# Respreading one image's convolution, statistics and group norm over the sampling of the image before it

## The reference, cut to what matters

```python
# block 1: x = x + L0(gn(x))
xh = conv1x1(gn(x), w_in, b_in)                    # 64 -> 128 channels
kernels = kg_w2 @ relu(kg_w1 @ mean(xh) + kg_b1)   # 9 taps per image and channel
y = depthwise_conv3x3(xh, kernels)
y = y * tanh(softplus(y))
x = x + conv1x1(y, w_out, b_out)
# block 2: x = x + L1(gn(x)); gn: mean and variance of two channels over the image
offset, mask = conv3x3(gn(x)), sigmoid(conv3x3(gn(x)))
val = bilinear samples of gn(x) at 9 offset taps per pixel, times mask
z = conv1x1([conv(val, w_def), offset, mask]); x = x + silu(batchnorm(z))
```

## Time and profile before

| | us |
|---|---|
| median of 3 runs | 5547.52 (5545.2 to 5550.46) |
| the profiled execution | 5541.43 |
| its span, first to last instruction | 5539.6 |
| PE busy (81% of the span) | 4466.2 |
| DVE busy (81%) | 4498.5 |
| ACT busy (47%) | 2595.6 |
| POOL busy (73%) | 4041.9 |

### The profile page before, as it was taken

One profiled execution on the slowest core, in us unless ns is written; L12 is line 12 of the kernel. 1 busy time (PEld: TensorE's weight loads), 2 busy tenths in 40 slices (PEclk: granted clock), 3 DMA queues, 4 the chain that ended last, 5 costly groups with the idle time before them and its releaser, 6 DMA issues.

```text
span 5539.6 us, 46074 instructions
## 1 busy us (share of the span) xinstructions
PE 4466.2 (81%) x14774; PEld 1996.3 (36%) x14774; DVE 4498.5 (81%) x5310; ACT 2595.6 (47%) x3580; POOL 4041.9 (73%) x4243
## 2 busy tenths in 40 slices
PE   8688787888878888788887878887778887888874
PEld 3233343433434333333333433333333343333331
DVE  6888969888797887978879798897978879788765
ACT  3354445445445544444554454454445444445321
POOL 1777777777777777777777777777777777777776
PEclk8687878888787887878878788788888878788886
DMA  4334344343534435344343443434344353433433
GB/s 106 103 118 135 103 133 122 120 131 105 141 111 131 123 109 143 104 131 123 116 136 105 133 123 120 133 103 139 115 132 123 110 144 105 131 115 114 122 107 101
DMA packets 280991, 667.35 MB, mean 120 GB/s; under 512 B 76191, under 2 KB 118058, under 8 KB 278506
## 3 DMA queue, kind: packets, MB, share of 16 engines
q0 software_dynamic: 203328, 555.49, 33.7%
q1 hardware_dynamic: 77424, 108.93, 7.9%
HBM read 610.00 MB, written 54.12 MB: 120 GB/s over the span
## 4 chain that ended last, share of the span: by engine, by line
PE 36%; DVE 25%; POOL 22%; issue 12%; ACT 3%; DMA 2%; DVEq 0%; POOLq 0%; SPq 0%; ACTq 0%
POOL gat L504 22%; PE yo_ps L774 12%; PE tap_ps L774 7%; DVE gat L1371 5%; PE z_ps L696 5%; DVE pairs L1350 5%; DVE conv_ps L1241 4%; DVE hat_s L1398 4%; PE tap_ps L690 2%; DMA gat<-patch_table,ixu 2%; PE conv_ps L588 2%; PE conv_ps L568 2%; DVE uc L1248 1%; PE xh_ps L756 1%; DVE conv_ps L1238 1%
## 5 line engine op out<-in xcount | busy, mean ns | idle before, releaser
L504 POOL DMA_INDIRECT gat<-patch_table,ixu x4236 | 4033.6, 952 | 1483.6 <-issue 1261.8
L1371 DVE TENSOR_TENSOR gat<-gat,wgt_ps 128x1024 f32<-128x1024 f32 x1059 | 1283.9, 1215 | 445.9 <-DMA gat<-patch_table,ixu 438.7
L1350 DVE TENSOR_REDUCE pairs<-gat 128x256 f32<-128x1024 f32 x1024 | 1239.4, 1210 | 0.0
L774 PE MATMUL yo_ps<-hat_s,hat_image 128*128 128x512 f32 x1860 | 1007.0, 695 | 7.0 <-issue 7.0
L774 PE MATMUL tap_ps<-hat_s,hat_image 128*128 128x512 f32 x1860 | 895.1, 631 | 0.0
L690 PE MATMUL tap_ps<-ident,pairs 128*128 128x128 f32 x2048 | 393.3, 324 | 572.6 <-DVE pairs L1350 572.4
L1039 ACT ACTIVATE val<-tap_ps 128x512 f32<-128x512 f32 x512 | 303.3, 592 | 1087.9 <-PE tap_ps L690 1087.7
L774 PEld LDWEIGHTS yo_ps<-hat_s,hat_image 128*128 128x128 f32 x1860 | 417.5, 232 | 603.5 <-issue 594.2
L1241 DVE SCALAR_TENSOR_TENSOR conv_ps<-xh,kb,conv_ps 128x1024 f32<-128x1024 f32 x480 | 617.5, 1286 | 12.7
L690 PEld LDWEIGHTS tap_ps<-ident,pairs 128*128 128x128 f32 x2048 | 271.1, 163 | 886.1 <-DVE pairs L1350 716.9
L774 PEld LDWEIGHTS tap_ps<-hat_s,hat_image 128*128 128x128 f32 x1860 | 360.5, 202 | 427.6 <-issue 417.8
(11 more groups left out here) (238 smaller groups left out, 4858.2 us busy)
## 6 DMA issues: line engine op xcount, KB each, us to landing
gat<-patch_table,ixu POOLq DMA_INDIRECT x4236, 2.7
xb<-in_x SPq DMA_DIRECT2D x31, 1024.0 KB, 10.8
patch_table<-rec SPq DMA_DIRECT2D x120, 256.0 KB, 2.6
hat_image<-patch_table SPq DMA_DIRECT2D x144, 128.0 KB
out<-n_z SPq DMA_DIRECT2D x128, 128.0 KB, 2.4
patch_table<-np SPq DMA_DIRECT2D x2, 1072.5 KB
patch_table<-gat SPq DMA_DIRECT2D x8, 256.0 KB, 2.0
patch_table<-rec SPq DMA_DIRECT2D x16, 97.0 KB
```

The source lines that it names most:

```text
L504: pool.indirect_dma_start(gat[:, k, t * 2 * REC:(t + 1) * 2 * REC], None, table_rows, bass.IndirectOffsetOnAxis(ixu[:, i, k, t:t + 1], 0)) ...
L774: m = pe.matmul(hat_sums[t % 2][:, :], hat_image[:, q // NCH % 2, i, t, :], hat_s[:, i, :], start=(i == 0), stop=(i == HI - 1))
L1350: dve.tensor_reduce(total, gat[:, k, :].rearrange("p (t x c h) -> p t c x h", t=TILES, x=2, h=2), mybir.AxisListType.XY, ALU.add).then_inc ...
L1371: dve.tensor_tensor(patch, patch, wk.rearrange("p (n h) -> p n h", h=2).unsqueeze(2).to_broadcast([128, TILES * 2, C, 2]), ALU.mult).then_ ...
```

## The change

Of one image's steps in the chunks of the image before (steady state, images 1 to 15):

- chunk 0: rows of `convolve 0` at units 1, 2 and 4 instead of 2, 3 and 5; `exp`, `ln`, `tanh` of pair 0 at 5, 6, 7; `project 0` at 8 instead of unit 1 of chunk 1.
- chunk 1: `residual 0` alone (its statistics go to chunk 2), three rows of `convolve 1` at 2, 4 and 7, `exp 1` at 8.
- chunk 2: `ln 1`, `tanh 1`, `project 1` at 1, 2, 3, `residual 1` and `statistics 0` at 5, two rows of `convolve 2` at 6 and 8.
- chunk 3: the last row of `convolve 2` at 1, its activation and `project 2` at 2 to 5, `statistics 1`, `residual 2` at 7, the first row of `convolve 3` at 8.
- chunk 4: two rows of `convolve 3` at 1 and 2, activation and `project 3` at 3 to 6, `statistics 2`, `residual 3`, `statistics 3`, and `group_mean` at the end. Before, chunks 0 to 3 held one whole pair each, and chunk 4 the rest and the whole group norm.
- chunk 5: `group_var` and `normalise` at 1 and 2; `last_row` and `offsets 0` at 4 instead of 1; the rest of the preparation moves behind, so that `to_pixels 1` and `to_table 4` pass to chunk 6.
- chunk 7 stays.

In the prologue PE does five of the nine taps instead of six, ACT instead of DVE clips at 20 out of the bank, the activations have four buffers, the statistics and kernels of image 1 go behind the first index, the table uses three banks instead of two, and five copies instead of six are DVE's. `store_last` becomes two transfers: 96 partitions, each with one run of 1024 bytes, and one partition.

```diff
-PE_TAPS = 6
+PE_TAPS = 5
-PLAN_FIRST = ((2, "convolve 0"), (3, "convolve 1"), (5, "convolve 2"), (6, "exp"), (7, "ln"), (8, "tanh"))
-PLAN_BLOCK0 = ((1, "project"), (3, "residual"), (3, "convolve 0"), (4, "convolve 1"), (5, "convolve 2"), (6, "exp"),
-               (7, "ln"), (8, "tanh"), (8, "finish"))
+PLAN_CONV = (
+    ((1, "convolve 0 0"), (2, "convolve 0 1"), (4, "convolve 0 2"), (5, "exp 0"), (6, "ln 0"), (7, "tanh 0"), (8, "project 0")),
+    ((1, "residual 0"), (2, "convolve 1 0"), (4, "convolve 1 1"), (7, "convolve 1 2"), (8, "exp 1"), (8, "finish")),
+    ((1, "ln 1"), (2, "tanh 1"), (3, "project 1"), (5, "residual 1"), (5, "statistics 0"), (6, "convolve 2 0"), (8, "convolve 2 1"), (8, "finish")),
+    ((1, "convolve 2 2"), (2, "exp 2"), (3, "ln 2"), (4, "tanh 2"), (5, "project 2"), (6, "statistics 1"), (7, "residual 2"), (8, "convolve 3 0"),
+     (8, "finish")),
+    ((1, "convolve 3 1"), (2, "convolve 3 2"), (3, "exp 3"), (4, "ln 3"), (4, "statistics 2"), (5, "tanh 3"), (6, "project 3"), (8, "residual 3"),
+     (8, "statistics 3"), (8, "finish"), (KK, "group_mean")),
+)
...
-PLAN_NORM = ((1, "project"), (3, "residual"), (4, "group_mean"), (5, "group_var"), (6, "normalise"), (8, "finish"))
 PLAN_PREPARE = (
-    ((1, "last_row"), (1, "offsets 0"), (2, "to_table 0"), (2, "x_stats 0"), (3, "to_table 1"), (4, "offsets 1"), (4, "to_pixels 0"),
-     (5, "to_table 2"), (5, "x_stats 1"), (6, "to_table 3"), (7, "to_pixels 1"), (8, "to_table 4"), (8, "finish")),
-    ((1, "offsets 2"), (2, "to_table 5"), (2, "points 0"), (3, "offsets 3"), (3, "to_pixels 2"), (4, "points 1"), (4, "to_table 6"),
-     (5, "x_stats 2"), (5, "to_table 7"), (6, "points 2"), (6, "to_pixels 3"), (7, "x_stats 3"), (8, "finish")),
+    ((1, "group_var"), (2, "normalise"), (2, "x_stats 0"), (4, "last_row"), (4, "offsets 0"), (5, "to_table 0"), (5, "x_stats 1"), (6, "to_table 1"),
+     (7, "offsets 1"), (7, "to_table 2"), (8, "to_pixels 0"), (8, "finish"), (KK, "to_table 3")),
+    ((1, "to_table 4"), (1, "offsets 2"), (2, "to_pixels 1"), (3, "to_table 5"), (3, "points 0"), (4, "offsets 3"), (4, "to_table 6"), (5, "points 1"),
+     (5, "to_pixels 2"), (5, "to_table 7"), (5, "x_stats 2"), (6, "points 2"), (7, "to_pixels 3"), (7, "x_stats 3"), (8, "finish")),
...
-                dst = table_rows[bass.ds((n % 2) * (TR * PW) + PIX, 2 * LAST), :].rearrange("(t p) d -> p t d", p=LAST)
-                sp.dma_start(dst, rec_l.rearrange("p (t d) -> p t d", t=2)).then_inc(last_out, 16)
+                first = (n % 2) * (TR * PW) + PIX
+                dst = table_rows[first:first + 2 * (LAST - 1), :].rearrange("(p t) d -> p (t d)", t=2)
+                sp.dma_start(dst, rec_l[0:LAST - 1, :]).then_inc(last_out, 16)
+                dst = table_rows[first + 2 * (LAST - 1):first + 2 * LAST, :].rearrange("(p t) d -> p (t d)", t=2)
+                sp.dma_start(dst, rec_l[LAST - 1:LAST, :]).then_inc(last_out, 16)
...
+            for s in range(NCH // 2):
+                project(0, s, s)
...
+            group_mean(0)
+            group_var(0)
+            first_table(0)
+            first_table(1)
+            offsets(0, 0, 0)
+            last_row(0)
+            for c in range(2, 6):
+                first_table(c)
+            first_pixels(0, 0)
+            first_table(6)
+            first_table(7)
+            x_mean(1)
             x_var(1)
             x_norm(1)
-            group_mean(0)
-            group_var(0)
```

More of the change, by code:

```diff
@@ L115, in plan_of @@
 def plan_of(b, g):
[L117 to L122, removed]
+    plan = PLAN_CONV[g] if g < 5 else PLAN_PREPARE[g - 5]
+    if b == 0 and g < len(PLAN_START):
+        plan = by_unit(plan, PLAN_START[g])
     q = b * NCH + g
@@ L138, in group @@
             done = units
-        name, _, number = step.partition(" ")
+        name, *numbers = step.split()
         if name in steps:
-            steps[name](b, g, int(number or 0))
+            steps[name](b, g, *(int(i) for i in numbers))
     if done < KK:
@@ L1153, in _, with hidden @@
             dve.memset(one_c[:, :], 1.0).then_inc(consts_set, 1)
-            def hidden(n, s):
-                for j in range(2):
+            def hidden(n, s, lo=0, hi=2):
+                for j in range(lo, hi):
                     q = n * NCH + s * 2 + j
@@ L1220, in convolve_first @@
                         dve.scalar_tensor_tensor(acc, src, kb[:, k:k + 1], acc, ALU.mult, ALU.add).then_inc(conv, 1)
[L1221 to L1225 removed]
+                    if k == 0:
+                        hidden(0, NCH // 2 - 1, 1, 2)
             def convolve(n, s, row):
@@ L1262, in residual, with statistics @@
                     dve.scalar_tensor_tensor(own, project_ps(n, j)[:, :], b_out, own, ALU.add, ALU.add).then_inc(x1_done, 1)
+                if n == 0:
+                    statistics(0, s)
+            def statistics(n, s):
+                for j in range(2):
+                    q = n * NCH + s * 2 + j
                     dve.wait_ge(x1_done, q + 2)
-                    dve.bn_stats(stat1[:, bass.ds(s * 2 + j, 1), :].rearrange("p o s -> p (o s)"), own).then_inc(st_done, 1)
+                    dve.bn_stats(stat1[:, bass.ds(s * 2 + j, 1), :].rearrange("p o s -> p (o s)"), xb[:, n % 2, span(s * 2 + j)]).then_inc(st_done, 1)
             def group_mean(n):
@@ L1419, in _ @@
             x_norm(0)
-            for s in range(NCH // 2):
+            for s in range(NCH // 2 - 1):
                 hidden(0, s)
+            hidden(0, NCH // 2 - 1, 0, 1)
             kernels(0)
-            for s in range(NCH // 2):
-                convolve_first(s, s % 2)
-                if s > 0:
-                    project(0, s - 1, (s - 1) % 2)
-                if s > 1:
-                    residual(0, s - 2)
-                x_stats(1, s)
-            x_mean(1)
-            residual(0, NCH // 2 - 2)
-            project(0, NCH // 2 - 1, 1)
+            convolve_first(0)
+            convolve_first(1)
+            x_stats(1, 0)
+            project(0, 0, 0)
+            convolve_first(2)
+            project(0, 1, 1)
+            x_stats(1, 1)
+            convolve_first(3)
+            project(0, 2, 2)
+            residual(0, 0)
+            residual(0, 1)
+            project(0, 3, 3)
+            residual(0, 2)
+            residual(0, 3)
+            group_mean(0)
             step = [0]
@@ L1457, in _ @@
             dve.sem_inc(set_dve, 1)
-            x_var(1)
-            residual(0, NCH // 2 - 1)
-            x_norm(1)
             dve.wait_ge(border_out, 32)
-            group_mean(0)
             group_var(0)
+            x_stats(1, 2)
             normalise(0)
-            for c in BY_DVE:
+            first_table(1)
+            dve.wait_ge(set_pe, 1)
+            then(dve.tensor_copy(w_pair[:, :, :].rearrange("p k c -> p (k c)"), tap_ps[0][:, 0:PAIRS * C]))
+            then(dve.tensor_copy(w_single, tap_ps[0][0:C, PAIRS * C:GROUPS * C]))
+            then(dve.tensor_copy(w_hat[:, :], tap_ps[0][:, GROUPS * C:(GROUPS + 1) * C]))
+            dve.sem_inc(set_dve, 1)
+            x_stats(1, 3)
+            for c in BY_DVE[1:]:
                 first_table(c)
             first_points(0)
+            x_mean(1)
+            x_var(1)
+            x_norm(1)
             kernels(1)
```

186 lines of the change are left out of this document (81 added, 105 removed).

## The result

The changed kernel takes 5686.84 us (median of 4 runs, 5676.02 to 5706.32), the kernel before 5546.36 beside it: ratio 1.026, 95% interval 1.0245 to 1.0274. The profiled execution took 5684.62 us, its span is 5682.8 (before 5539.6).

A forecast was written before the change was run, and what follows sets the result against it. POOL's gather pace bounds the kernel, 330 of 337.2 us an image. Loop 345.2, +8.0 an image: +112 over fourteen, -8 for prologue and image 0, 5645 profiled, median 6.1 above: 5651 us; range 5585 to 5765.

The forecast's parts named there:

- The late norm decides: Chunks 5 to 7: later group norm puts hat_part 60 us after chunk 5's start; to next chunk 0 140.5 us, before 136.5.
- the sum: Loop per image: 207 us for chunks 0 to 4 plus 140.5 us for 5 to 7, 347.5; less 2.3, 345.2.
- The spread chunks: Chunks 0 to 4 on DVE with rows spread: together 207 us, before 202.0.
- The clock: PE, less idle, would be at its higher clock more often: 2.3 us taken off each image.
- The prologue: Ahead of image 0: group mean 8 us earlier, first gather at 107 to 110 us; 8 us gain left after image 0.
- The lag's limit: POOL at chunk 0: waits begin once DVE's first step trails POOL's first gather by more than 24.3 us.
- DVE's slack: DVE's waits for landings in chunks 4 and 5, 19.3 us an image, would fall well below that.
- The waits vanish: Rival: loop through DVE stays below POOL's 330 us, transpose waits go; 5464 us, 5490 with a third left; chance 0.24.
- drain: ACT's table loads: a skill's 1.38 us after each 1.28 us switch; the trace showed none, so none was counted.

The follow-up runs named there:

- the run with the points early: Second chunk's offsets, pixels and points ahead of image 1's hidden layer, against the changed kernel with the previous loop plan: 5532.14 us, 0.9978 of the kernel before.
- rows spread inside their chunk: Rows of convolutions 1 to 3 at units 3, 5, 7 instead of 3, 4, 5, against the changed kernel with the previous loop plan: 5460.16 us.

## Why the prediction was right, and where its steps were off

It gave 5651 us and slower; measured are 5686.84, 36 us more, inside the range and the forecast's own bounds. For the profiled execution it is 39 us (5684.62 for 5645): 34 in the loop (14 x 2.4) and 6 in image 0; the median stands 2 us above this execution and not 6.

- *The late norm decides.* Right: with the preparation behind it, it makes the whole loss, 7.5 us by the norm and 3.2 by the later places, for which the sum had no term. Its end was put at 13 us into chunk 5 (12.9). The way from there was mis-sized: `hat_part` at 60 us, measured 64.6 in image 5 (64.5 in the mean). I shortened the way because `to_pixels 1` leaves it, though I had noted that `points 0`, which waits for it, stands ahead of `hat_part` on DVE. That is half of the miss: with the points moved behind it `hat_part` still begins at 62.2 (mean), held by `hat_g`. From `hat_part` to chunk 7 27 us, measured 27.1; chunk 7 53.5, measured 53.2.
- *The spread chunks.* 46 to 47, 41, 42, 39.5 and 37.5 us, together 207; measured 44.7, 40.7, 43.0, 38.9, 36.6, together 203.9. Chunk 0 was put too long by 2: DVE waited for `xh` for 1.4 us of the 2.5 (image 5). Against this chunks 5 to 7 take 144.0 us in the mean and not 140.5. That the sum of 347.5 meets 347.6 is luck: one part is 3.1 us too long, the other 3.5 too short.
- *The clock.* I took 2.3 us an image off because PE would be at its higher clock more often. No row gave this number. The mean granted clock went from 0.815 to 0.822: over images 1 to 13 from 0.864 to 0.878 in chunks 0 to 4, but from 0.756 to 0.758 in chunks 5 to 7, where the longer chain stands. So it did not rise where the loss is. What it gave in chunks 0 to 4 is inside their 203.9 us, and no run parts it from them. Without it the loop would have been met, by the luck above.
- *The prologue.* The group mean is at 81.9 us, 10.0 earlier (8 expected), the first gather at 104.0, not 107 to 110. For image 1 I took 8 us, and 2 were left, below my 3. The text itself said that DVE begins chunk 0 at 146 as before (145.5); the run with the points early shows that this decides: DVE 8.9 us earlier there brings image 1 10.4 us earlier.
- *The lag's limit.* 24.3 us at chunk 0. With a measured lag of 34.4 POOL should lose 10.1 there, and its chunk 0 takes 51.7 us instead of some 40.3, 11.4 more: right within 1.3 us. The waits are over 150 us (281) and long at chunk 1, but not at chunk 5, where it is 2.9 (1.3 before).
- *DVE's slack.* Its waits for landings fall to 11.0 us in image 5 (19.3 before). Right.
- *The rivals.* "The waits vanish" (5464) described what rows spread inside their chunk do: with the norm left early the kernel runs at 5460, with an image at 332.0. What the prediction missed is that spreading and the late norm can be had apart. The change's own rows, which cross a chunk's border, are another matter: they lose at `project` what they win at the hat products. No run has them with an early norm, nor the rows of units 3, 5 and 7 with a late one.

On table loads the sum was right to carry no drain: in the changed kernel, too, ACT's next activation starts 0.01 us after the load's 1.28 us (timeline of ACT, chunk 5, image 5), and the load 0.02 us after the activation before it, where the Trainium skill (ScalarE: Activation LUTs, "What ACT_TABLE_LOAD costs") adds a drain of 1.38 us.

```profile
2097.53 1.28 ACT L1051 ACT_TABLE_LOAD   x1
2098.82 1.13 ACT L1051 ACTIVATE n_z<-z_ps,bn_shift,bn_scale 64x256 f32<-64x256 f32 x2
```

## What to carry to other kernels

Where engines walk one hand-written order, spread long operations between the step that feeds another engine and the step that waits for it, and leave the head of a serial chain where it is: here a chain that starts 16 us later costs 7.5 us an image with the rows bunched, and the spread rows of the change don't win it back. When a wait is moved out of the way, read what stands at the same unit of the same queue before hoping for it; it took the whole wait here. A producer that starts earlier gained 1 us of 15 here, as its consumer started when it did: trace what the consumer waits for first.

## What the runs showed that I had not expected

- 2.9 us of DVE's wait in each of three chunks were worth 77 us (14 x 5.5), since they pushed the lag over a limit that POOL feels only two chunks later; 5 us of wait in chunk 6 were worth nothing.
- The lag at which POOL begins to lose depends on where the rows of chunk 0 stand. Taking POOL's chunk 0 less 40.2 us as lost: with rows at units 1, 2 and 4 it is 22.8 to 22.9 us (lag 29.6 with 6.8 lost, 34.4 with 11.5), with rows at 2, 3 and 4 or 5 it is 28.2 to 28.4 (35.2 with 7.0, 31.6 with 3.2).
- The first gather 15 us earlier, or 5 us by the store, left the total within 0.2%.
